# TensorE loads the block and slot numbers of 18 groups at once, not of 3

## The reference, cut to what matters

```
_sage_conv (3 times):  msg_sum = segment_sum(h[src], dst);  h @ W_self + msg_sum / deg @ W_neigh + b
attention layer:       alpha = softmax over dst of leaky_relu(a_src[row] + a_dst[col]);  out = segment_sum(xt[row] * alpha, col)
Runge-Kutta layer:     f(y) = segment_sum(y[src3] * e3, dst3);  k1 .. k4 from four calls of f
relation layer:        msg = (x @ W_rel)[src, etype] * norm;  relu(segment_sum(msg, dst) + bias + x @ loop_weight)
```

## Time and profile before

| | us |
|---|---|
| median of three runs | 13578.29 (13573.32 to 13611.32) |
| profiled execution | 13585.59 |
| its span in the trace | 13583.8 |
| PE busy | 10090.9 (74%) |
| DVE busy | 7971.0 (59%) |
| POOL busy | 6409.9 (47%) |
| ACT busy | 3712.1 (27%) |

### The profile page before, as it was taken

The page is one execution under the profiler, slowest core; times in us unless marked ns, Lnnn a source line. Parts: engine busy times, 40 slices in busy tenths (PEclk is TensorE's granted clock), DMA queues, the critical chain, the costliest instruction groups (busy, mean ns, idle before and its releaser), DMA issues.

```text
span 13583.8 us, 192267 instructions
## 1 busy us (share of the span) xinstructions
PE 10090.9 (74%) x68184; PEld 8162.2 (60%) x68289; DVE 7971.0 (59%) x13503; ACT 3712.1 (27%) x6670; POOL 6409.9 (47%) x6626
## 2 busy tenths in 40 slices
PE   6796067758665788764689868986998699899444
PEld 3675067657654333454688768876887688644333
DVE  8754066436444888777688646764676477600334
ACT  0242040220313577532332033203320332154000
POOL 0277776777773677300045603460455045501776
PEclk8665599989988999998999999999999999999555
DMA  1000087556663333322799768876887688776222
GB/s 54 2 4 18 16 269 227 177 182 190 207 194 107 110 106 107 88 81 81 248 310 314 203 214 281 294 203 215 287 287 204 215 294 272 244 297 254 53 53 56
DMA packets 1073032, 2382.23 MB, mean 175 GB/s; under 512 B 199212, under 2 KB 385888, under 8 KB 1045028
## 3 DMA queue, kind: packets, MB, share of 16 engines
q0 software_dynamic: 354208, 926.60, 25.0%
q10 hardware_dynamic: 403392, 811.55, 17.0%
q1 hardware_dynamic: 314564, 632.22, 13.1%
HBM read 1211.29 MB, written 1158.47 MB: 174 GB/s over the span
## 4 chain that ended last, share of the span: by engine, by line
PE 39%; POOL 26%; issue 15%; DVE 11%; DMA 7%; ACT 1%; DVEq 1%; ACTq 0%; POOLq 0%; SPq 0%
PE ps L2024 15%; PE ps L2044 14%; POOL list L739 6%; POOL list_f L739 6%; POOL rows_work L760 6%; POOL rows_work L771 5%; PE ps L2134 5%; POOL rows_work L795 3%; DMA rows_work<-messages_R,rows_R 2%; DVE rows_work L1507 2%; DMA rows_work<-near 2%; DMA rows_work<-messages_F,rows_R 2%; PE ps L1957 1%; PE ps L2036 1%; DMA ADM<-near 1%
## 5 line engine op out<-in xcount | busy, mean ns | idle before, releaser
L2024 PE MATMUL ps<-H,onehot 128*128 x23760 | 3191.4, 286 | 1038.2 <-DVE rows_work L1507 535.3
L795 POOL DMA_INDIRECT rows_work<-messages_F,rows_R x1890 | 1828.1, 967 | 4038.5 <-DMA messages_F<-rows_work 2640.3
L2024 PEld LDWEIGHTS ps<-H,onehot 128*128 128x128 f32 x23760 | 2905.3, 196 | 1243.9 <-issue 1174.4
L2044 PE MATMUL ps<-rows_work,onehot 128*128 128x128 f32 (+1 forms) x15840 | 2157.0, 282 | 329.6 <-DMA rows_work<-messages_F,rows_R 193.1
L932 ACT CAST onehot<-rows_work 128x512 f32<-128x512 uint8 x1980 | 1222.5, 618 | 3818.9 <-PE ps L2024 2515.0
L2044 PEld LDWEIGHTS ps<-rows_work,onehot 128*128 128x128 f32 x15840 | 1951.6, 192 | 496.8 <-issue 446.8
L1507 DVE TENSOR_TENSOR rows_work<-ps,list_words 128x512 f32<-128x512 f32 x2160 | 1484.4, 688 | 847.3 <-PE ps L2024 847.0
L1515 DVE TENSOR_TENSOR onehot<-ps,list_words 128x512 f32<-128x512 f32 x1980 | 1355.7, 688 | 599.4 <-PE ps L2044 581.3
L760 POOL DMA_INDIRECT rows_work<-rel_table,rows_F x832 | 788.0, 947 | 967.6 <-DMA rel_table<-list_words 714.4
L739 POOL DMA_INDIRECT list<-list_words,rows_R x831 | 812.9, 978 | 849.3 <-DVE rows_R L1273 576.2
L795 POOL DMA_INDIRECT rows_work<-messages_R,rows_R x1080 | 1021.1, 946 | 388.0 <-issue 261.7
(11 more groups left out here) (350 smaller groups left out, 10981.2 us busy)
## 6 DMA issues: line engine op xcount, KB each, us to landing
messages_F<-rows_work ACTq DMA_DIRECT2D x630, 792.0 KB
messages_R<-rows_work ACTq DMA_DIRECT2D x360, 792.0 KB
rel_table<-list_words SPq DMA_DIRECT2D x196, 1024.0 KB, 3.8
rows_work<-onet SPq DMA_DIRECT2D x480, 192.0 KB
gat_rows<-rows_work SPq DMA_DIRECT2D x220, 264.0 KB, 2.1
rows_work<-gat_rows SPq DMA_DIRECT2D x220, 264.0 KB, 2.7
ADM<-onet SPq DMA_DIRECT2D x240, 192.0 KB
rows_work<-near SPq DMA_DIRECT2D x180, 192.0 KB
```

What stands on the lines that cost most here:

```text
L795: pool.indirect_dma_start(out=ring2[:, G2 % RING2, :], out_offset=None, in_=rows_dram[PASSES[r]], in_offset=bass.IndirectOffsetOnAxis(ap=t ...
L2024: ins = mm(ps[:, G1 % 3, j * P:(j + 1) * P], onet_f[G1 % 2][:, j * P:(j + 1) * P], hflat[:, bass.ds(at["blocks"][g % GPW], FEAT)], start=T ...
L2044: ins = mm(into, member, ring2[:, G2 % RING2, j * AUX:j * AUX + width], start=False, stop=True, skip_group_check=True)
```

## The change

In the messages and the sums of the 11 passes, PE loads the words of six windows (`NAMED`) at once at every 18th group, 18 words in `message_group` and 12 in `sum_group`, and the matmuls pick their register from that longer list. In the attention layer it loads the seven words of each of four windows (`LOOKED`) at once, 28 words, and the first words of four windows, not of two. In the relation layer the two loads of a window change places in the program and stay else as they were. The 90 windows make 15 loads in a pass, where there were 90.

```diff
--- before.py
+++ after.py
@@ -103,6 +103,8 @@
 RUN = 4
 GROUP = P * RUN
 CELLS = BLOCKS * BLOCKS
+NAMED = 6
+LOOKED = 4
 GPW = 3
 WIN = -(-(((EDGES + (RUN - 1) * CELLS) // RUN) // P + BLOCKS) // GPW)
 GROUPS = GPW * WIN
@@ -526,10 +528,10 @@
                 skip_runtime_bounds_check_because="each is AUX times a count of BLOCKS - 1 comparisons")
             return values
 
-        def slots_of(engine, key, w):
+        def slots_of(engine, key, w, n=1):
 
             _, values = nc.values_load_multi_w_load_instructions(
-                slot_of[key][:, w * TABLE + 1:w * TABLE + WINDOW], engines=(engine,),
+                slot_of[key][:, w * TABLE:(w + n) * TABLE].rearrange("o (w j) -> o w j", j=TABLE)[:, :, 1:WINDOW], engines=(engine,),
                 min_val=0, max_val=2 * 512 + AUX,
                 skip_runtime_bounds_check_because="each block has a tile, so that eight tiles in a row are of eight blocks in a row at most")
             return values
@@ -552,7 +554,7 @@
         def window_words(engine, n, w, words):
 
             _, values = nc.values_load_multi_w_load_instructions(
-                windows_of[n][:, w * WTAB + words.start:w * WTAB + words.stop], engines=(engine,),
+                windows_of[n].rearrange("o (w j) -> o w j", j=WTAB)[:, w:w + min(NAMED, WIN - w), words], engines=(engine,),
                 min_val=0, max_val=(BLOCKS - 1) * FEAT if words.start == 0 else (GPW - 1) * AUX,
                 skip_runtime_bounds_check_because="each is FEAT or AUX times a count of BLOCKS - 1 comparisons, or of the blocks in three groups in a row")
             return values
@@ -1920,8 +1922,12 @@
                 ins.then_inc(rel_mixed, 1)
 
             def look_up(name, w, offsets):
-                places = places_of(mybir.EngineType.PE, name[-1], w) if name != "gat F" else None
-                offsets["next"] = slots_of(mybir.EngineType.PE, name[-1], w), places
+                if name != "gat F":
+                    offsets["next"] = slots_of(mybir.EngineType.PE, name[-1], w), places_of(mybir.EngineType.PE, name[-1], w)
+                    return
+                if w % LOOKED == 0:
+                    offsets["looked"] = slots_of(mybir.EngineType.PE, name[-1], w, min(LOOKED, WINDOWS - w))
+                offsets["next"] = offsets["looked"][w % LOOKED * (WINDOW - 1):(w % LOOKED + 1) * (WINDOW - 1)], None
 
             def sum_quad(name, w, second, width, offsets):
 
@@ -1933,8 +1939,8 @@
                     offsets["slots"], offsets["places"] = offsets["next"]
                     if adds(name):
                         pe.wait_ge(window_stored, m0 + w - 1)
-                    elif w % 2 == 0:
-                        offsets["firsts"] = firsts_of(mybir.EngineType.PE, key, w, 2)
+                    elif w % LOOKED == 0:
+                        offsets["firsts"] = firsts_of(mybir.EngineType.PE, key, w, min(LOOKED, WINDOWS - w))
 
                     cleared = SLOTS * AUX // SLOT_BANKS
                     for k in range(SLOT_BANKS):
@@ -1960,7 +1966,7 @@
 
                     if m0 + w:
                         pe.wait_ge(window_stored, m0 + w)
-                    mm(half[:, 0:width], ident[:, :], sums_flat[:, bass.ds(offsets["firsts"][w % 2], width)],
+                    mm(half[:, 0:width], ident[:, :], sums_flat[:, bass.ds(offsets["firsts"][w % LOOKED], width)],
                        start=False, stop=True, skip_group_check=True).then_inc(window_summed, 1)
 
             def block_sums(name, width=FEAT):
@@ -2010,8 +2016,9 @@
             def message_group(m, g, at):
 
                 G1, w = GROUPS * m + g, g // GPW
+                if g % (NAMED * GPW) == 0:
+                    at["blocks"] = window_words(mybir.EngineType.PE, "FR".index(PASSES[m]), w, slice(0, GPW))
                 if g % GPW == 0:
-                    at["blocks"] = window_words(mybir.EngineType.PE, "FR".index(PASSES[m]), w, slice(0, GPW))
                     step_no = (m - SAGE) // 2
                     if m < SAGE and (3 * w + 2) // GB < GI:
                         pe.wait_ge(h_ready, 1 + (GI * (m - 1) + (3 * w + 2) // GB + 1 if m else 0))
@@ -2022,15 +2029,16 @@
                     pe.wait_ge(messages_scaled, G1 - 2)
                 for j in range(RUN):
                     ins = mm(ps[:, G1 % 3, j * P:(j + 1) * P], onet_f[G1 % 2][:, j * P:(j + 1) * P],
-                             hflat[:, bass.ds(at["blocks"][g % GPW], FEAT)], start=True, stop=True)
+                             hflat[:, bass.ds(at["blocks"][g % (NAMED * GPW)], FEAT)], start=True, stop=True)
                 ins.then_inc(messages_made, 1)
 
             def sum_group(r, g, at):
 
                 G2, w, W2, n = GROUPS * r + g, g // GPW, WIN * r + g // GPW, 1 - "FR".index(PASSES[r])
                 bank = ps[:, 3 + W2 % 2, :]
+                if g % (NAMED * GPW) == 0:
+                    at["slots"] = window_words(mybir.EngineType.PE, n, w, slice(3, 5))
                 if g % GPW == 0:
-                    at["slots"] = window_words(mybir.EngineType.PE, n, w, slice(3, 5))
                     if W2 >= 2:
                         pe.wait_ge(group_added, W2 - 1)
                     mm(bank[:, 0:WSUM].rearrange("p (a b) -> p a b", a=4), naught[:, :],
@@ -2040,7 +2048,7 @@
                 for j in range(RUN):
                     member = member_f[G2 % 3][:, j * P:(j + 1) * P]
                     width = AUX if r in WITH_AUX else FEAT
-                    into = bank[:, 0:width] if g % GPW == 0 else bank[:, bass.ds(at["slots"][g % GPW - 1], width)]
+                    into = bank[:, 0:width] if g % GPW == 0 else bank[:, bass.ds(at["slots"][w % NAMED * (GPW - 1) + g % GPW - 1], width)]
                     ins = mm(into, member, ring2[:, G2 % RING2, j * AUX:j * AUX + width], start=False, stop=True, skip_group_check=True)
                 ins.then_inc(group_summed, 1)
```

## The result

The changed kernel takes 13820.76 us (median of four runs, 13812.77 to 13842.13) against 13577.67 us; the ratio is 1.0169 (95% interval 1.0153 to 1.0186). It is slower, as forecast, and inside the range, but by 243 us where the forecast had 90: the sum was off by more than its own size. The profiled execution has a span of 13823.4 us.

The account below looks back on a forecast made before the run. No engine was full: PE's register loads bound messages alone, PE mixed passes, POOL sums alone. Messages alone -210, mixed +240, attention +60 made +90 us on 13585.6, 13676, or 13668 against the median; range 13440 to 13850.

Parts of the forecast that it names:

- Price of a load: PE's register loads: 12 words 2.86 us, 18 words 4.26 us, 28 words 6.59 us, without any wait at the message store.
- the surplus: Extra load time where a window's message store has just started: 1.6 us for three words, 1.7 for two, counted once a load.
- Rival 2: Cheap words: 18 words read at the 1286 ns of sixteen, exposed time nearly gone, about -480 us, 13100; chance 0.08.
- rival 3: Extra load time at the message store paid by the word: 14.2 us for 18 words, 14800 or so; chance 0.10.
- rival 4: The gathered load is split into small ones as registers run short: no change, 13580; chance 0.02.
- rival 1: A load once in six windows no longer meets the message store: net -130 us, about 13470; chance 0.20.
- the line: Straight-line price of PE's register loads: about 67 ns and 233 ns a word.
- Passes 5, 7, 9: Messages alone: six windows fall from 28.0 to 24.6 us, taken as -50 us for each pass.
- Passes 1 and 2: Messages alone: 0 to the end, as POOL's list sets when the first gather of the sums comes.
- Mixed: Four passes bound by PE: long loads of slots and blocks leave idle and some half clock, 60 us a pass, +240 us.
- Attention: Attention sums: one load of 6.59 us for four windows, 5.4 exposed against 3.26 before, +60 us.
- Passes 0 and 3: Messages alone, gain capped by POOL's list and the DMA in pass 0, DMA and a stop in pass 3: -35 and -25 us.

Follow-up runs that it names:

- e8: Kernel before, with blocks and slots of two windows loaded at once (6 and 4 words), attention layer as before: 13750.24 us, ratio 1.0113.
- e1: Kernel before, with only the block offsets of the messages loaded for six windows at once: ratio 1.0069, on a slower chip.
- e2: Kernel before, with only the slot offsets of the sums loaded for six windows at once: ratio 1.0067, on a slower chip.
- e5b: Changed kernel, with DVE's making of the one-hot bytes in passes 0 and 3 moved behind the scalings: 13724.95 us, ratio 1.0094 against the kernel before.
- e6: Kernel before, small loads kept, with the making of the one-hot bytes in passes 0 and 3 moved behind the scalings: 13588.87 us, ratio 0.9991.
- e7: Kernel before, with PE's three-word load of blocks made for the next window, behind the window's first group: 13262.83 us, ratio 0.9750.
- e9: Kernel before, with small block and slot loads a window ahead, behind the first group, and one-hot bytes of passes 0 and 3 made behind the scalings: 13097.82 us.
- e4: Kernel before, with block offsets of six windows loaded at once only in passes 5, 7 and 9: 13446.09 us, ratio 0.9889.
- e11: Kernel before, all loads in place, with ACT starting the store of messages one group earlier: 13204.4 us, ratio 0.9705.
- e10: As e9, but the load of blocks reads all eight words of a window's entry in place of three: 13047.06 us, ratio 0.9589.

## Why the forecast was wrong, point by point

- **Price of a load**: right. 233 ns a word holds up to 28 words (6.84 us against 6.59), and the surplus is paid once a load: 5.98 us for 18 words in pass 5, 3.09 for six in e8, 2.38 for three. Rival 2 (cheap words) and rival 3 (a surplus by the word) fall by the same rows; rival 4 (split loads) too, with 15 loads a pass; and rival 1 (no surplus) by the 5.98 us, which is 1.7 above the line.
- **Passes 5, 7, 9**: right to 1 us. PE's timeline of pass 7 shows 5.1 us of idle, as worked out:

```profile
9499.73 9.15 PE L2031 MATMUL ps<-H,onehot 128*128 x74
9513.99 13.25 PE L2031 MATMUL ps<-H,onehot 128*128 x94 [5.11 <-issue]
```

- **Passes 1 and 2**: right. They are 53 and 45 us shorter, and the sums behind them start 908.7 us after pass 0's end for pass 1, where it was 909.1: the gain is POOL's.
- **Mixed**: the sum is right (+225 against +240), but in part by luck. The load of slots was put at 4.56 us with a gap of 2.5; in the third mixed pass it takes mostly 3.2 to 3.8 us and leaves 2.1 us and less. The load of blocks was put at 4.26 us without a surplus; it takes 5.4 to 6.3, but starts with more work queued, so that the idle is 3.5 to 4.5 us (forecast 3.4). Half clock follows 13 of its 14 stops in that pass, not one in three. The too dear slots and the too cheap clock cancel. Each part alone (e1, e2) has the load and the gap of the forecast. Two of these stops:

```profile
9904.58 0.33 PE L2044 MATMUL ps<-naught 128*128 128x396 bf16 x1 [1.72 <-issue]
...
9932.41 1.05 PE L2052 MATMUL ps<-rows_work,onehot 128*128 128x128 f32 x8
9937.01 1.80 PE L2031 MATMUL ps<-H,onehot 128*128 x8 [3.55 <-issue]
9938.61 1.91 PE L2052 MATMUL ps<-rows_work,onehot 128*128 128x128 f32 x8
...
9944.85 0.33 PE L2044 MATMUL ps<-naught 128*128 128x396 bf16 x1 [1.48 <-issue]
```

Not counted was the start of each mixed pass, where the long load of blocks leaves 6.4 us of idle ahead of the third one's first matmul, against 2.0 before: +20 us in four.
- **Attention**: +48 of 60, with both terms too small. The stop is 6.61 us and not 5.4. The small stops it replaces are longer, too: 1.47 us for nearly every load of seven words, 5.9 us in four windows, where I had taken 3.26 from the pieces of the chain. The row of the kernel before, then that of the changed one:

```profile
5894.25 1.16 PE L1957 MATMUL ps<-rows_work,onehot 128*128 128x132 f32 x8 [1.47 <-issue]
...
5919.63 2.12 PE L1963 MATMUL ps<-rows_work,onehot 128*128 128x132 f32 x8 [6.61 <-issue]
```

That is +0.7 us for four windows, some 20 us of the 48 (an estimate from these two rows). The granted clock went from 0.91 to 0.85 over the stretch; how the rest divides isn't shown.

- **Passes 0 and 3: the step that failed.** The working took 3.0 us for each window without a load, and let only the DMA's share and POOL's list cap the gain: -35 and -25. They became +40.5 and +38.0, 139 us of the 150 that the forecast is short of. A window without a load doesn't come down to 3.0 us there: DVE's wait for the DMA of the one-hot bytes, a term the working left out, holds it at 4.2. PE's timeline in pass 0 of the changed kernel:

```profile
1873.74 3.09 PE L2031 MATMUL ps<-H,onehot 128*128 x24 [1.16 <-DVE rows_work L1505]
1877.85 3.09 PE L2031 MATMUL ps<-H,onehot 128*128 x24 [1.02 <-DVE rows_work L1505]
1882.21 3.09 PE L2031 MATMUL ps<-H,onehot 128*128 x24 [1.26 <-DVE rows_work L1505]
1890.74 8.04 PE L2031 MATMUL ps<-H,onehot 128*128 x48 [5.44 <-issue]
1900.99 7.40 PE L2031 MATMUL ps<-H,onehot 128*128 x48 [2.21 <-DVE rows_work L1505]
1909.05 3.09 PE L2031 MATMUL ps<-H,onehot 128*128 x24 [0.65 <-ACT onehot L934]
```

Windows without a load have gaps of 1.0 to 1.3 us: 4.2 us a window and not 3.0. The stop of 5.4 us is added to that in full, with half clock behind it. What keeps them, DVE's line shows:

```profile
1912.03 1.02 DVE L1495 TENSOR_SCALAR rows_work<-rows_work,part 128x1536 uint8<-128x1536 uint8 x1 [2.02 <-DMA rows_work<-near]
...
1912.96 1.88 DVE L1505 TENSOR_SCALAR rows_work<-ps 128x512 f32<-128x512 f32 x3
```

DVE waits 2.02 us for the bytes of two windows ahead, and then scales three groups in a row, which PE had begun at 1909.05 and left by 1912.1; PE needs their banks and starts again at 1913.88. During PE's stop the DMAs can't run further ahead either: the program has each wait until ACT has widened the window that its buffer held, and ACT stands still with PE. The row was there to be read in the kernel before, under what DVE waited for in 350 us of pass 0:

```profile
DVE rows_work L1493 <- DMA rows_work<-near: 90.5, 51, 3.1
DVE ADM L1493 <- DMA ADM<-near: 44.3, 26, 2.9
```

135 us of waits in 77 windows, 1.75 us in each, in an engine that PE's gaps are named after the earlier trace rows. I set that name aside for pass 1, rightly, since there the load ends the gap, and carried it over to pass 0, where DVE has a wait of its own. e5b, e6, e7 and e9 show it from both sides. What they don't explain is the rest: with DVE's work moved (e5b) the two passes are 8 and 9 us shorter than in the kernel before, not 35 and 25, so that 43 of the 139 us stay open. ACT waits 48.6 us in 340 us of pass 0 there for DVE to make the bytes, and the DMA share is 0.81; no run separates these.

## What to carry to other kernels

To gather small stops into one long stop is no gain in itself: it saves what is paid per stop (here the surplus: e4, 1.1% faster), and pays with the clock and with every chain whose buffers are freed by the stopped engine. Before a stall is removed, look in each stage for the wait of the next engine that lies beside it, and cap the gain by the period that this one allows. And where a short instruction takes three times its usual duration in some stages, ask what runs at that moment: moving the instruction, or the other work, by one group was worth 2.5 to 3% here, and gathering lost 1.7%.

## What the runs showed of the hardware

- A register load of PE took 0.77 us for three words undisturbed and 2.38 us (median, pass 5) where it started 0.76 us behind the issue of the store of messages. With the store issued one group earlier (e11) it took 1.8 us at 1.4 us behind the issue and 1.05 us at 2.2 us behind it. In the third mixed pass the load of two words went from 2.24 to 1.30 us (medians; undisturbed 0.53).
- Eight words in a row from the start of an entry took 587 ns at the least (e10), three words 767 ns (e7); 12 words took 2.93 us and 28 words 6.84 us.
- With an idle of 2.25 us at each of 45 loads in 417 us (pass 7 of e8) TensorE's granted clock was 0.86; with gaps of about 1.5 us at 90 loads in 420 us (before) it was 0.98.
- The same kernel took 13578 to 13605 us on some chips and 16290 us on another, where sums alone took 394 to 401 us and not 334 to 338, and pass 0 over 720 us and not 412.
